# Scan layers on one Trainium2 core: two products into a free PSUM bank between the first norm's spreading and the projection in

## What is computed

```
h     = layernorm(x, n1_g, n1_b)
p     = h @ w_in + b_in                                   # 96 -> 192
local = depthwise_conv_3x3(p, k_conv)                     # 9 taps
lr, rl, tb, bt = EMA scans of local along rows and columns, both ways
mixed = layernorm(0.25 * (lr + rl + tb + bt) + local, on_g, on_b)
x     = x + (mixed @ w_out + b_out)                       # 192 -> 96
h2    = layernorm(x, n2_g, n2_b)
x     = x + (gelu(h2 @ w1 + b1) @ w2 + b2)                # 96 -> 384 -> 96
```

## Time and profile before

| what | us |
|---|---|
| median of three runs | 3518.51 |
| the profiled execution, its own time | 3515.43 |
| its span, first to last instruction | 3513.3 |
| scan layers within the span | from about 3074 to 3513 |
| slots 2 to 7 within the span | from about 3119 to 3388 |

### The profile page before, as it was taken

One profiled execution on the slowest core, in us unless ns is written; L12 is line 12 of the kernel. 1 busy time (PEld: TensorE's weight loads), 2 busy tenths in 40 slices (PEclk: granted clock), 3 DMA queues, 4 the chain that ended last, 5 costly groups with the idle time before them and its releaser, 6 DMA issues. The chain is left out here.

```text
span 3513.3 us, 136148 instructions
## 1 busy us (share of the span) xinstructions
PE 3044.4 (87%) x50244; PEld 2300.0 (65%) x50244; DVE 2527.1 (72%) x12097; ACT 1814.5 (52%) x5570; POOL 1031.7 (29%) x2514
## 2 busy tenths in 40 slices
PE   5459999999958667999999999999999999568987
PEld 1136666666613226888988888988888898445654
DVE  4639999999956337777777777777777777668882
ACT  1249999999903035444544444544444454234443
POOL 0028777877700001222222222222222222100000
PEclk9669999999968875555555555555555555579899
DMA  1243333333220000000000000000000000000000
GB/s 34 84 139 110 109 99 100 111 109 112 84 83 0 16 2 3 5 5 5 4 5 5 5 5 5 5 5 5 5 5 5 5 5 5 13 1 1 1 5 14
DMA packets 54609, 116.11 MB, mean 33 GB/s; under 512 B 12314, under 2 KB 19802, under 8 KB 53693
## 3 DMA queue, kind: packets, MB, share of 16 engines
q1 hardware_dynamic: 37104, 53.42, 5.4%
q0 software_dynamic: 13824, 50.34, 4.0%
q10 hardware_dynamic: 2956, 3.15, 0.4%
HBM read 84.06 MB, written 22.81 MB: 30 GB/s over the span
## 5 line engine op out<-in xcount | busy, mean ns | idle before, releaser
L504 PE MATMUL g_zr<-g_hp,g_wp 97*128 97x4 f16 x24576 | 1077.0, 171 | 49.3 <-issue 49.0
L504 PEld LDWEIGHTS g_zr<-g_hp,g_wp 97*128 97x128 f16 x24576 | 951.2, 108 | 156.3 <-issue 51.3
L612 POOL COPY s_y<-g_hs 96x8 f32 x2048 | 401.0, 196 | 1357.1 <-DVE g_hs L555 1357.1
L595 ACT ACTIVATE g_e<-g_tn 96x8 f32<-96x8 f32 x2048 | 439.3, 214 | 555.5 <-DVE g_tn L540 555.5
L480 PE MATMUL g_zr<-s_inner,g_wi 96*128 (+2 forms) x6240 | 586.0, 234 | 49.0 <-issue 26.8
L553 DVE TENSOR_TENSOR_SCAN g_hp<-g_gates,g_e 96x16 f16<-96x16 f32 x2048 | 383.9, 187 | 324.2 <-ACT g_e L595 218.3
L592 ACT ACTIVATE g_gates<-g_zr 96x16 f32<-96x16 f32 x2048 | 400.3, 195 | 305.7 <-PE g_zr L504 304.7
L868 DVE CUSTOM_DVE_ANT_0 a_negated<-a_scores,a_mask 128x1024 f32<-128x1024 f32 x384 | 468.1, 1219 | 84.7 <-DMA a_mask<-in_L_mask 44.0
L511 PE MATMUL g_n<-g_hp,g_wp 97*128 97x8 f16 x8192 | 520.2, 174 | 0.0
L894 ACT ACTIVATE a_probs<-a_negated,a_negmax 128x1024 f32<-128x1024 f32 x384 | 442.3, 1152 | 25.3 <-DVE a_negmax L868 15.5
L540 DVE TENSOR_TENSOR_SCAN g_tn<-g_gates,g_n 96x24 f32<-96x24 f32 x2048 | 386.3, 189 | 82.1 <-ACT g_gates L592 82.1
(11 more groups left out here) (319 smaller groups left out, 3278.1 us busy)
## 6 DMA issues: line engine op xcount, KB each, us to landing
a_mask<-in_L_mask POOLq DMA_DIRECT2D x96, 512.0 KB, 5.5
a_k<-k_rows SPq DMA_DIRECT2D x96, 144.0 KB
q_rows<-r_q_parts SPq DMA_DIRECT2D x12, 576.0 KB, 7.2
k_rows<-r_k_parts SPq DMA_DIRECT2D x12, 576.0 KB, 7.2
a_q<-q_rows SPq DMA_DIRECT2D x96, 72.0 KB
o_parts<-a_o_sb SPq DMA_DIRECT2D x384, 18.0 KB
o_part<-o_parts SPq DMA_DIRECT2D x32, 192.0 KB
out_x<-x SPq DMA_DIRECT2D x4, 384.0 KB, 3.0
```

The source lines that it names most:

```text
L504: mm = pe.matmul(zr_bank[u, k][:, 1 - g, d, :, at], wp[0:97, part, (2 * u + d) * NG + g, :], hp[u][0:97, d * NB:(d + 1) * NB, e], start=False,
L595: act.activation(e1[u][:, :, 0], tn[u][:, :, 2], ACT.Tanh, scale=to_tanh).then_inc(n_and_zh[u], 1)
L612: po.tensor_copy(yv[:, 2 * u:2 * u + 2, :, bass.ds(token, 1)], h.unsqueeze(3)).then_inc(y_ok[u], 1)
```

## The change

In PE's stream, between the spreading of the first norm's factors and the first half of the projection in, two products of 96 x 97 weights with 512 columns are issued wherever stage e is there as well. They write `mix[1]`, and nothing reads what they write: `mix_tile(1)` starts its accumulation anew over it. A wait for `e_copied` stands ahead of them from e = 1 on. Both stages are there in six slots, so twelve products, 24 records, are added. Nothing is removed or moved, and no other engine's stream is touched.

```diff
                         if h and m is not None:
                             pe.wait_ge(m_rooted, m + 1)
                         spread_half(ring[h], h, f_parts, f_spread)
+                    if e is not None:
+                        if e:
+                            pe.wait_ge(e_copied, 2 * e)
+                        for h in range(2):
+                            pe.matmul(mix[1][0:R, bank(h)], centre[:, :], f_squares[0:C, bank(h)], start=True, stop=True)
                     project_in(f, 0)
                 if e is not None:
                     turn_pairs(e, range(6, 8))
```

## The result

The changed kernel takes 3527.07 us (median of ten runs, 3524.37 to 3528.53) against 3518.48 (ten runs, 3515.30 to 3520.27): a ratio of 1.0024 with a 95% interval of 1.0015 to 1.0034, so slower by 8.6 us. The time lies in the predicted range of 3514.5 to 3528.5 and 4 us above the predicted 3523.0. It is over the bound of 0.2%, by 1.6 us; the interval reaches from 0.15 to 0.34%, so that the loss is clear and its place against that bound is not.

A forecast was written before the change was run, and what follows sets the result against it. DVE was taken to set the pace between spreading and scans, PE from the scans on. Slot 5's -2.45, the scans' +6.1 and slot 2's +0.8 gave +4.5 us on 3518.5: 3523.0 us, range 3514.5 to 3528.5.

The forecast's parts named there:

- rival A: The forecast itself: the clock falls ahead of the scans in most of slots 3 to 7; +4.5 us, chance 0.50.
- the three outcomes: Whole kernel against the one before: slower by over 0.2% 0.18, within 0.2% 0.76, faster by over 0.2% 0.06.
- What bounds: Slots 3 to 7: DVE sets the pace between spreading and scans, PE from the scans on; 21.56 us turns to scans.
- The products fit in the gap at no cost: Ahead of the projection in, slots 3 to 7: four records take 1.88 us, 0.5 us to spare, cost 0.
- The gap no longer lets the clock fall: Ahead of the projection in: idle shrinks from 2.24 to about 0.5 us, clock holds; gain 2.45 us in slot 5.
- The slack moves ahead of the scans: Slots 3 to 7: PE's idle time ahead of the scans grows from 1.45 to about 2.9 us.
- The price there: Scans to projection down: low clock costs 1.52 us a slot, in four of slots 3 to 7, 6.1 us.
- rival C: From mix_tile(0) on, slots 3 to 7: low clock stays through most scans, 2.76 us a slot; +12.2, 3530.7 us; chance 0.13.
- Slot 2: Products at the low clock delay the projection, and scans start 0.8 us late; cost 0.8 us, ends 0 and 1.8.
- Slots 8 to 11: Slots not touched by the change, though the clock's falls may shift; put at 0, 1.5 us either way.
- The sum: Whole kernel: -2.45 + 6.1 + 0.8 = +4.5 us, carried to the median as 3523.0 us.
- slot 2's 2.27 us: A pause in slot 2 over which the clock held, set against the expectation that all five slots pay.

## Why the prediction held, and where it was off

The time lies in the range, and the chain of the forecast came out: the gap filled, the clock held there, the pause moved ahead of the scans, the clock fell in it. The size did not. It was nearly twice the sum and over the upper end of rival A (3519.5 to 3525.5), and of the three outcomes it was slower by over 0.2%, which had been given 0.18.

*What bounds.* Right. DVE's centring sets the start of the scans, PE what comes after. Turns to scans take 21.56 us with and without the change in slot 4 (3230.34 - 3208.77 = 21.57), and what the scans lose reaches the next slot (2.67 us lost, the slot 47.79 - 45.12 = 2.67 longer).

*The products fit in the gap at no cost.* Right: 1.91 us against 1.88, 0.50 us left against 0.5.

*The gap no longer lets the clock fall, worth 2.45 us in slot 5.* Right in all five slots; with the pause filled as well, slot 5 lasts 45.23.

*The slack moves ahead of the scans.* Right: 3.10 us against about 2.9.

*The price there.* **This is the term that was off**: 1.52 us a slot in four slots of five, 6.1 us. It was 2.67 us in all five, 13.3 us. The step took slot 9 as the nearest row, by the length of its pause, and left slot 8's 2.76 to rival C. Slot 9's clock falls just as its scans begin, and is back 3.4 us later; in the change it falls about 1 us before them and stays low for 6.8. Both prices occur in these kernels with the same pause of 3.10 us: 1.56 us in slot 6 of the kernel with the products cut to 8 columns, 2.67 in the change. So the length of the pause doesn't decide the price.

Slot 9 shows it best. Its code and its pause of 2.93 us are the same in every kernel but the two that fill it, and yet in the kernel with the two products cut to 8 columns it took 3474.38 - 3454.50 = 19.88 us from scans to projection down, against 18.68 in the kernel before and 18.50 in the change:

```profile
3454.50 3.70 PE L1567 MATMUL e_mix<-e_along_rows,e_tokens 128*96 128x128 f32 x16 [2.93 <-DVE e_tokens L1808]
...
3474.38 5.31 PE L1689 MATMUL e_ring<-e_hidden,l_w 128*97 128x512 f32 x12
```

There the clock fell at 3453.5, 1.0 us ahead of the scans, and was low for 6.8 us. What goes with the price, in all profiles here and behind pauses of 2.1 to 3.1 us in slots 3 to 7 and 9, is the moment of the fall: where the clock fell 1.0 to 2.1 us ahead of the scans, it stayed low for 6.8 us and cost 2.2 to 2.7; where it fell at most 0.6 us ahead, or once they had begun, it stayed low for 3.4 us and cost 1.3 to 1.6. What sets that moment was not found. The prediction's one row for this price had fallen late.

*Slot 2.* Expected 0.8, measured 0.00 in the first profile and 0.68 in the second. The mechanism was wrong in both: the scans were to start 0.8 us late, and they start 18.13 and 18.12 us behind the slot's first turns, against 18.13 before. In the first profile the clock came back at about 3130.3 and the products took 2.74 us rather than 3.4, so the projection ran fast and made up for them. The 0.68 of the second come from a clock that fell ahead of the scans, as in the slots behind it. That they lie near 0.8 is luck.

*Slots 8 to 11.* Put at 0 with 1.5 either way, measured -0.6.

*The sum.* +4.5 predicted, +11.2 between the two profiled executions, +8.6 between the medians. The two differ because the first profiled execution of the kernel before lay 3.05 us under its median, and that of the changed kernel 0.38. From the first product of the scan layers to the end it is 439.2 and 439.7 us in the two profiles of the kernel before, 449.6 and 450.2 in those of the change, so +10.4 in either pair, while the start of the scan layers lies anywhere from 3073.1 to 3077.0 in these four. Set on the median before, 10.4 would be 3528.9, just outside the range. Why the medians are only 8.6 apart isn't shown; that the time lies inside the range is in part luck.

*Which rival.* By its size the outcome lies between A and C. By the signs that the prediction gave for the changed profile it is C, with 0.13 as its chance: L1567 and L1571 are both slow, 3.70 and 3.93 us, and slots last 47.8 against C's 47.9 and A's 46.6. C's reason, that these short products bring the clock back late, isn't shown; in slot 9 of the kernel before it came back over the same products after 3.4 us. Rows at 1.52 and at 2.76 were both at hand, and the sum took only the lower.

The Trainium skill's TensorE: Matmul & The Clock Gate, in its part on HAM oscillation, tells of a kernel in which each burst behind a wait for data starts cold, once per tile. It tells this of waits of about 3 to 5 us, which the prediction left out when it set slot 2's 2.27 us against it. The trace of the change agrees: pauses of 3.10 us, and a fall in five slots of five, where the forecast took four. But falls came behind shorter pauses too, 2.24 us in the kernel before.

## What to carry to other kernels

Filling one idle gap of an engine that another engine paces does not remove the slack, it moves it; find where it comes out, and what stands behind it there. Here a slow projection was a free place to spend the low clock, and the scans were not. In this kernel two ways were left: fill every pause ahead of work that bounds the slot (3510.55 us), or leave the low clock where it costs nothing. The pauses to start with are those behind which the engine is the bound: slots 8 and 9 alone gave 5.1 us. And where one row is to price a low clock, look how long it lasted there and how much of it fell on work that bounds the slot; two rows with pauses of like length can differ by 1.2 us.

## What was unexpected of the hardware

The clock can fall behind a pause far shorter than the low clock that follows: behind 1.36 us of idle time ahead of the projection in slot 4 of the kernel with one product, four records took 3.47 us, against 1.96 in slot 3 behind 1.35 us. Over the same pause of 2.11 us the clock held once and fell four times.

The changed kernel is more regular than the one before: its slots 4 to 7 last 47.66 to 47.86 us in both profiles, with the same price in each, while kernels in which some gaps are left half filled have slots of 45.1, 46.7 and 47.7 side by side.

Products that nothing reads cost nothing measurable where PE waits anyway: 54 more records than the kernel before, in slots 2 to 7, gave a kernel that is some 0.1% faster.
